# Row normalisation and rounding moved from VectorE to ScalarE in the attention units of a cross-attention and feed-forward kernel

## The reference, cut to what matters

```python
def act_quant(x):
    scale = 127.0 / jnp.clip(jnp.max(jnp.abs(x), axis=-1, keepdims=True), 1e-05)
    return jnp.clip(jnp.round(x * scale), -128, 127) / scale
...
# x: (1, 2048, 256); ctx_1024: (1, 1601, 256), masked; 4 heads of 64
x = x + xattn(ctx_1024, layernorm(x), mask, ...)   # keys and values from context and latents, softmax, W_out, bias
x = x + ffn(layernorm(x), w1, conv_w, conv_b, w2)  # bit_linear, depthwise conv of 3, silu, bit_linear
```

## Time and profile before

| | |
|---|---|
| median of 3 runs | 434.38 us (434.12 to 435.97) |
| the profiled execution | 434.61 us, of which the span from first to last instruction is 432.8 us |
| granted TensorE clock | 0.995 of full, mean over the span |
| PE busy | 404.0 us (93%) |
| DVE busy | 376.7 us (87%) |
| ACT busy | 313.9 us (73%) |
| POOL busy | 81.8 us (19%) |
| the chain that ended last | PE 49%, DVE 28%, ACT 16%, issue 3%, DMA 2% |

### The profile page before, as it was taken

How to read it: one execution, slowest core, us unless ns; L and a number is a source line. 1 busy time by engine, 2 the same in 40 slices (tenths; PEclk the granted TensorE clock), 3 DMA queues, 4 the chain that set the end, 5 groups by cost and what they waited for, 6 DMA issues and landing times.

```text
span 432.8 us, 13955 instructions
## 1 busy us (share of the span) xinstructions
PE 404.0 (93%) x5983; PEld 277.2 (64%) x5983; DVE 376.7 (87%) x604; ACT 313.9 (73%) x368; POOL 81.8 (19%) x109
## 2 busy tenths in 40 slices
PE   6999997899999999999999999999999977999894
PEld 5666674566666676676666666666676735676573
DVE  5789987977887899799799799799799899999993
ACT  2466777589979766766767767766766688999974
POOL 3287775500000020020020020020020010221200
PEclk9999999999999999999999999999999998999999
DMA  7825323711111111111111211211111000001002
GB/s 227 219 25 107 54 41 43 231 53 64 52 39 64 39 44 57 51 39 63 51 39 50 64 39 38 64 50 39 40 38 39 2 0 2 2 26 48 27 27 79
DMA packets 28688, 24.63 MB, mean 57 GB/s; under 512 B 6278, under 2 KB 28367, under 8 KB 28623
## 3 DMA queue, kind: packets, MB, share of 16 engines
q1 hardware_dynamic: 26106, 21.59, 15.6%
q0 software_dynamic: 2176, 2.10, 3.7%
q10 hardware_dynamic: 340, 0.01, 0.0%
HBM read 9.00 MB, written 2.10 MB: 26 GB/s over the span
## 4 chain that ended last, share of the span: by engine, by line
PE 49%; DVE 28%; ACT 16%; issue 3%; DMA 2%; ACTq 0%; DVEq 0%; SPq 0%
DVE arena L719 17%; PE sc L1714 10%; ACT arena L1302 5%; PE heads L1731 5%; PE heads L1732 4%; PE heads L1733 4%; PE heads L1537 4%; PE sc L1549 3%; ACT qq L1389 3%; PE sc L1814 2%; PE by L1618 2%; ACT qq L1397 2%; PE bx L1549 2%; PE by L1549 2%; ACT kk L1367 1%
## 5 line engine op out<-in xcount | busy, mean ns | idle before, releaser
L719 DVE SCALAR_TENSOR_TENSOR arena<-arena 128x1024 bf16<-128x1024 f32 x160 | 190.9, 1221 | 29.4 <-ACT arena L1302 28.2
L1302 ACT ACTIVATE arena<-sc,kb 128x1024 f32<-128x1024 f32 x160 | 169.9, 1115 | 60.9 <-PE sc L1714 60.7
L1731 PEld LDWEIGHTS heads<-v,arena 128*128 128x128 bf16 x1280 | 117.1, 97 | 41.3 <-issue 27.2
L1731 PE MATMUL heads<-v,arena 128*128 128x65 f16 x1280 | 129.8, 194 | 4.7 <-DVE arena L719 4.3
L1732 PE MATMUL heads<-v,arena 128*128 128x64 f16 x1280 | 128.9, 195 | 0.0
L1733 PE MATMUL heads<-v,arena 128*128 128x65 f16 x1280 | 128.4, 192 | 0.0
L1714 PE MATMUL sc<-qs,kst 64*128 64x512 f16 x960 | 118.0, 378 | 2.4 <-DVE kk L661 1.5
L1732 PEld LDWEIGHTS heads<-v,arena 128*128 128x128 bf16 x1280 | 118.7, 97 | 0.1
L1733 PEld LDWEIGHTS heads<-v,arena 128*128 128x128 bf16 x1280 | 118.8, 99 | 0.0
L1714 PEld LDWEIGHTS sc<-qs,kst 64*128 64x128 f16 x960 | 40.1, 94 | 47.7 <-issue 4.3
L528 POOL TENSOR_SCALAR frs<-fmv 128x2 f32<-128x2 f32 x8 | 8.0, 997 | 250.6 <-DVE fmv L793 250.6
(11 more groups left out here) (209 smaller groups left out, 582.7 us busy)
## 6 DMA issues: line engine op xcount, KB each, us to landing
kst<-kk SPq DMA_DIRECT2D x80, 128.0 KB, 2.0
xs<-in_x SPq DMA_DIRECT2D x8, 256.0 KB, 5.1
xs<-in_L_xattn_b_out POOLq DMA_DIRECT2D x8, 256.0 KB, 5.8
qs<-qq SPq DMA_DIRECT2D x16, 128.0 KB, 2.5
out<-cbuf SPq DMA_DIRECT2D x7, 256.0 KB, 2.1
xs<-in_ctx SPq DMA_DIRECT2D x6, 256.0 KB, 5.7
xs<-in_L_ffn_w SPq DMA_DIRECT2D x1, 1024.0 KB, 6.8
cbuf<-in_L_ffn_w SPq DMA_DIRECT2D x1, 1024.0 KB, 9.1
```

Of the source, the lines that this page charges most:

```text
L719: e.scalar_tensor_tensor(out=rest[:, j, :, :], in0=prob[:, j, :, :], scalar=SHRINK, in1=probh[:, j, :, :], op0=ALU.mult, op1=ALU.subtract) ...
L1302: a_.activation(prob[:, j, :, :], sc[(j + 1) % 2][:, :, :], ACT.Exp, bias=kb[:, bass.ds(i * QUAD + j, 1)]).then_inc(exp_done[j], 1)
L1731: t_.matmul(o, hi, row[:, 0:OW], start=first and sub == 0, stop=False, skip_group_check=True)
```

## The change

On DVE, `row_normed` is replaced by `row_shift`, which makes -mean x reciprocal deviation for both tiles in one small operation; the two normalising operations and the two rounding operations are issued by ACT (`row_norm`, `row_rounding`) with this bias. DVE's remaining row steps stand one or two remainders later. On ACT the normalising pair stands ahead of the exponentials of quad 3, the rounding pair between the exponentials of its tiles 2 and 3. The same is written into the branch for other numbers of quads.

```diff
-            def row_normed(b):
+            def row_shift(b):
                 dve.wait_ge(s["rstd2_ready"], b + 1)
                 settle(b)
-                for t in range(2):
-                    last = e.tensor_scalar(y[:, t, :], tile_of(b, t), fmv[:, t, 0:1], frs[:, 1, t:t + 1], ALU.subtract, ALU.mult)
-                last.then_inc(s["row_step"], 1)
+                e.scalar_tensor_tensor(out=fq[:, 3, 0:2], in0=fmv[:, 0:2, 0], scalar=-1.0, in1=frs[:, 1, 0:2], op0=ALU.mult, op1=ALU.mult).then_inc(s["row_shifted"], 1)
 
             def row_largest(b):
-                dve.wait_ge(s["row_step"], 7 * b + 1)
+                dve.wait_ge(s["row_normed"], b + 1)
+                settle(b)
                 e.tensor_reduce(fq[:, 0, 0:2], y, AX.X, ALU.max, apply_absolute_value=True).then_inc(s["row_step"], 1)
...
             def row_inverse(b):
-                dve.wait_ge(s["row_step"], 7 * b + 3)
-                e.reciprocal(fq[:, 2, 0:2], fq[:, 1, 0:2]).then_inc(s["row_step"], 1)
-
-            def row_rounded(b):
-                dve.wait_ge(s["row_step"], 7 * b + 4)
-                settle(b)
-                for t in range(2):
-                    last = e.tensor_scalar(y[:, t, :], y[:, t, :], fq[:, 2, t:t + 1], ROUND, ALU.mult, ALU.add)
-                last.then_inc(s["row_step"], 1)
+                dve.wait_ge(s["row_step"], 4 * b + 2)
+                e.reciprocal(fq[:, 2, 0:2], fq[:, 1, 0:2]).then_inc(s["row_inverted"], 1)
 
             def row_scaled_back(b):
-                dve.wait_ge(s["row_step"], 7 * b + 5)
+                dve.wait_ge(s["row_rounded"], b + 1)
...
                 remainder(first + 2, 0)
                 remainder(first + 2, 1)
+                row_shift(b)
                 remainder(first + 2, 2)
-                row_normed(b)
                 remainder(first + 2, 3)
+                remainder(first + 3, 0)
                 row_largest(b)
                 row_scale(b)
-                remainder(first + 3, 0)
+                remainder(first + 3, 1)
                 row_inverse(b)
-                remainder(first + 3, 1)
-                row_rounded(b)
                 remainder(first + 3, 2)
+                remainder(first + 3, 3)
                 row_scaled_back(b)
-                remainder(first + 3, 3)
                 row_high(b)
                 remainder(first + 4, 0)
                 row_low(b)
...
+            def row_norm(b):
+                act.wait_ge(s["row_shifted"], b + 1)
+                for t in range(2):
+                    last = a_.activation(y[:, t, :], xs[:, bass.ds(b * 2 + t, 1), :].rearrange("p a d -> p (a d)"), ACT.Identity, scale=frs[:, 1, t:t + 1], bias=fq[:, 3, t:t + 1])
+                last.then_inc(s["row_normed"], 1)
+
+            def row_rounding(b):
+                act.wait_ge(s["row_inverted"], b + 1)
+                for t in range(2):
+                    last = a_.activation(y[:, t, :], y[:, t, :], ACT.Identity, scale=fq[:, 2, t:t + 1], bias=shifts[:, 2:3])
+                last.then_inc(s["row_rounded"], 1)
+
             def unit(nq, b):
...
                 exponentials(first + 1, 1)
-                over(2, nq, lambda i: exponentials(first + i, i))
+                exponentials(first + 2, 2)
+                row_norm(b)
+                for j in range(QUAD):
+                    exponential(first + 3, 3, j)
+                    if j == 2:
+                        row_rounding(b)
+                over(4, nq, lambda i: exponentials(first + i, i))
                 rows_t(b)
```

More of the change, by code:

```diff
@@ L164, in xattn_ffn @@
         frs = sb("frs", [P, 2, 4], F32)
-        fq = sb("fq", [P, 3, 4], F32)
+        fq = sb("fq", [P, 4, 4], F32)
         fu = sb("fu", [P, 4, FT], F32)
@@ L239, in xattn_ffn @@
             rstd2_ready dq_ready xd_ps xd_ready h_ps edge_ps center_ready left_ready taps_done edge_step edge_done
-            u_ready row_step ut_ps scale_step scale_pool scale_back uscale_ready uscale_late uf_ready uqt_ps uq_ready uq_late0 uq_late1 o_ps res_ready pad_done passed""".split()
+            u_ready row_step row_shifted row_normed row_inverted row_rounded ut_ps scale_step scale_pool scale_back uscale_ready uscale_late uf_ready uqt_ps uq_ready uq_late0 uq_late1 o_ps res_ready pad_done passed""".split()
         s = {n: sem(n) for n in names}
@@ L793, in row_moments @@
                     e.bn_aggr(fmv[:, c0 + t, :], fst[:, c0 + t, :]).then_inc(s["prep_step"], 1)
-            def row_normed(b):
+            def row_shift(b):
                 dve.wait_ge(s["rstd2_ready"], b + 1)
                 settle(b)
-                for t in range(2):
-                    last = e.tensor_scalar(y[:, t, :], tile_of(b, t), fmv[:, t, 0:1], frs[:, 1, t:t + 1], ALU.subtract, ALU.mult)
-                last.then_inc(s["row_step"], 1)
+                e.scalar_tensor_tensor(out=fq[:, 3, 0:2], in0=fmv[:, 0:2, 0], scalar=-1.0, in1=frs[:, 1, 0:2], op0=ALU.mult, op1=ALU.mult).then_inc(s["row_shifted"], 1)
             def row_largest(b):
-                dve.wait_ge(s["row_step"], 7 * b + 1)
+                dve.wait_ge(s["row_normed"], b + 1)
+                settle(b)
                 e.tensor_reduce(fq[:, 0, 0:2], y, AX.X, ALU.max, apply_absolute_value=True).then_inc(s["row_step"], 1)
             def row_scale(b):
-                dve.wait_ge(s["row_step"], 7 * b + 2)
+                dve.wait_ge(s["row_step"], 4 * b + 1)
                 e.tensor_scalar(fq[:, 1, 0:2], fq[:, 0, 0:2], QUANT_EPS, 1.0 / 127.0, ALU.max, ALU.mult).then_inc(s["row_step"], 1)
             def row_inverse(b):
-                dve.wait_ge(s["row_step"], 7 * b + 3)
-                e.reciprocal(fq[:, 2, 0:2], fq[:, 1, 0:2]).then_inc(s["row_step"], 1)
-            def row_rounded(b):
-                dve.wait_ge(s["row_step"], 7 * b + 4)
-                settle(b)
-                for t in range(2):
-                    last = e.tensor_scalar(y[:, t, :], y[:, t, :], fq[:, 2, t:t + 1], ROUND, ALU.mult, ALU.add)
-                last.then_inc(s["row_step"], 1)
+                dve.wait_ge(s["row_step"], 4 * b + 2)
+                e.reciprocal(fq[:, 2, 0:2], fq[:, 1, 0:2]).then_inc(s["row_inverted"], 1)
             def row_scaled_back(b):
-                dve.wait_ge(s["row_step"], 7 * b + 5)
+                dve.wait_ge(s["row_rounded"], b + 1)
                 settle(b)
@@ L828, in row_high @@
             def row_high(b):
-                dve.wait_ge(s["row_step"], 7 * b + 6)
+                dve.wait_ge(s["row_step"], 4 * b + 3)
                 wait(dve, "xd_ps", b)
@@ L833, in row_low @@
             def row_low(b):
-                dve.wait_ge(s["row_step"], 7 * b + 7)
+                dve.wait_ge(s["row_step"], 4 * b + 4)
                 e.tensor_tensor(dq16[:, 1, :, :], y, dq16[:, 0, :, :], ALU.subtract).then_inc(s["dq_ready"], 1)
@@ L1161, in _ @@
                         remainder(first + 2, 1)
+                        row_shift(b)
                         remainder(first + 2, 2)
-                        row_normed(b)
                         remainder(first + 2, 3)
+                        remainder(first + 3, 0)
                         row_largest(b)
                         row_scale(b)
-                        remainder(first + 3, 0)
+                        remainder(first + 3, 1)
                         row_inverse(b)
-                        row_rounded(b)
-                        remainder(first + 3, 1)
+                        remainder(first + 3, 2)
+                        remainder(first + 3, 3)
                         row_scaled_back(b)
-                        remainder(first + 3, 2)
                         row_high(b)
-                        remainder(first + 3, 3)
+                        remainder(first + 4, 0)
                         row_low(b)
-                        with dve.Fori(4, nq) as i:
-                            remainders(first + i)
+                        for j in range(1, QUAD):
+                            remainder(first + 4, j)
+                        with dve.If(nq > XP // 2 + 1):
+                            with dve.Fori(5, nq) as i:
+                                remainders(first + i)
                 feed_forward()
```

## The result

The changed kernel takes 437.39 us (median; before in the same comparison 434.25), a ratio of 1.0082 with a 95% interval of 1.0063 to 1.0102: 3.6 us slower (2.7 to 4.4). The forecast was 438.5 us, slower by 4.1. The direction, the mechanism and its place came as predicted; the time lies inside the range.

A forecast was written before the change was run, and what follows sets the result against it. TensorE was taken as the bound nearly everywhere, with V4.1 setting the period; six units 0.68 us longer each gave 4.1 us, so 438.5 us, 0.95% slower, range 436.3 to 441.0 us for 8 in 10.

The forecast's parts named there:

- V4.1: TensorE's value products of quad 4, tile 1: claimed to set the unit's period and start 0.68 us later.
- The stall of 0.61 us per unit: TensorE's waits behind DVE in quads 3 and 4 before the change: 0.09 + 0.34 + 0.18 us per unit.
- The normalising pair is free: On ACT ahead of quad 3's exponentials: fits ACT's gap of 0.86 us; cost 0.03, at most 0.23.
- E3.0: ACT's exponential of quad 3, tile 0: claimed at 259.55 us, against 259.52 before.
- The shift's wait for POOL: DVE's shift in quad 2 waits for POOL's power until 257.63 us; hidden, since DVE waits until 257.68 anyway.
- The rounding pair: On ACT between quad 3's last two exponentials: idles 0.42 us for DVE's inverse, then holds ACT 1.00 us.
- E3.3: ACT's exponential of quad 3, tile 3: claimed to start at 264.93 us, 1.42 late.
- S4.1: TensorE's score products of quad 4, tile 1: claimed at 266.10 us instead of 265.41, waiting for a score bank.
- R3.3: DVE's remainder of the exponential of quad 3, tile 3: claimed at 266.07 us, after DVE idles 1.1 us.
- Faster: Rival: relieving DVE ends the stalls in quads 3 and 4, all 3.7 us comes back, 430.7 us; chance 0.09.
- No change: Rival: the two effects cancel, with quad 3's last exponential delayed near 0.75 us; 434.4 us; chance 0.06.
- Slower by more: Rival: POOL's late power delays the shift and the normalising pair too, 1.2 us per unit, 441.5 us; chance 0.05.

The follow-up runs named there:

- both eased: Changed kernel with the rounding pair behind quad 3's exponentials, and DVE's largest, reciprocal and low part each behind a later remainder; unit 32.47 us, 429.42 us, ratio 0.9910.
- DVE's order eased: Changed kernel, rounding pair left in place, DVE's high and low parts moved behind quad 4's remainders of tiles 0 and 1; unit 33.28 us, ratio 0.9982.

## Why the prediction was right

**The bound and the gate.** V4.1 set the end of the unit in both kernels, and the first five units repeat to 0.01 us (the last is 0.02 to 0.03 shorter). The stall of 0.61 us per unit that I took from the rows is borne out: the two runs without waits for remainders in quads 3 and 4 and with little or no wait at the scores are 0.59 and 0.66 shorter per unit than before.

**The normalising pair is free.** E3.0 was predicted at 259.55 on the clock of the rows before and came at 259.53 (263.32 less 3.79). The run with this half alone shows it at the end of the line: faster by 0.59 per unit.

**The shift's wait for POOL is hidden.** It stands in the waits with 0.60 us per unit, but DVE idled 0.62 in that place before, for an exponential; R2.2 comes 0.05 later (261.52 less 3.79 = 257.73). My sentence that a visible wait for POOL would show the prediction wrong was badly put: the wait is visible and harmless, because it took over an idle that was there.

**The rounding pair.** Every step of the working, on the same clock, predicted and seen: R3.0 260.68, 260.66; the inverse 263.74, 263.73; the pair 263.93, 263.92; E3.3 264.93, 264.92; S4.1 266.10, 266.07; R3.3 266.07, 266.05; scaled back 267.21, 267.19. The sign to look for was a wait of TensorE's scores of 0.7 us per unit; it reads 1.03 in the weight loads and 0.54 in the matmuls, and the scores start 0.66 late. The runs that move the pair show that this is cause and not company. One operation of the pair takes 594 ns in the units, as in the tail. The page "ScalarE: Activation LUTs" of the Trainium skill (Rules for kernel authors) gives an estimate of 0.51 us, for an operation with the bias alone as a pointer; here the scale is one as well. By the single operation its advice to keep such arithmetic on VectorE agrees with the traces, which have 594 ns on ACT and 407 ns on DVE for the normalising. For the kernel the advice is not borne out in this place: the normalising pair on ACT makes the unit 0.59 us shorter.

**The term that was mis-sized.** From the scaling back to the high part I took 0.52, as before; it is 0.64 (270.98 to 271.62). Before, a remainder stood between the two; now the second waits for the end of the first. This 0.12 is the difference between the 0.68 per unit predicted and the 0.80 measured, and it passes through every later step to V4.1, 271.19 where I had 271.08. Busy times were off as well: DVE's fell by 0.83 per unit (5 us in six, 7 forecast), and ACT's rose by 1.85 (11 us, 14 forecast), since I took the sum of durations that overlap.

**The sum.** The units alone lengthen by 6 x 0.80 = 4.8 us, more than the 4.1 forecast; the ratios say 3.6 and 2.3 us. A small part of the difference is seen at the end of the program, which the prediction took as moving as a whole. The last result on DVE, in the chain of waits before and after:

```profile
428.26 0.40 issue
428.66 0.48 DVE cbuf L957
```

```profile
433.52 0.04 issue
433.57 0.48 DVE cbuf L948
```

Between what released it and its start lie 0.40 us before, and 0.04 us in the changed kernel. This holds in both profiles of before and in all eight of kernels with a changed instruction list, whatever their speed, so about 0.4 us comes back that has nothing to do with row work: 4.8 - 0.4 = 4.4. Why the issue is quicker wasn't tried; the instruction list differs in its length on DVE and ACT, and no experiment took that apart. Reckoned so, the first ratio (3.6 us, at most 4.4) and those of the runs with either half of the change, with the rounding pair behind quad 3 and with both eased agree with their units.

Three ratios come out lower than their units say: the second one of the change (2.3 us for 4.4), the run with DVE's order eased (0.8 us faster for 0.5 slower) and the one with the pair one exponential earlier (9.1 for 11.2). All three were compared with the same 16 runs of before, which had the highest median of the three comparisons (434.73). In six of these 16 the mean granted clock was 0.985 to 0.991, and their median is 435.4; none of the 22 runs of the three kernels was below 0.994. Against the ten runs of before at 0.994 or more (median 434.16) the medians differ by 2.9, -0.2 and 9.9 us. So about 0.6 us of the lack goes with the clock, and the rest stays open.

That the time came within 1.1 us of the forecast is therefore in part luck: the units lengthened by 0.7 us more than was worked out, and the end of the program and the spread between runs took that back.

**The rivals.** "Faster" failed in the place that its deciding point named: E3.3's delay was 1.41, over 0.74; with the pair moved away from it, the gain that this rival promised is there in part (32.80), and in full with DVE's order eased too (32.47). "No change" needed a delay near 0.75 and fails by the same 1.41. "Slower by more" failed since POOL's power came in time: the shift started at 257.65 on the clock of the rows before (261.44 less 3.79). (Its sum, 434.4 + 6 x 1.2, is 441.6 and not 441.5; and "as much again" on both sides of 437.4 to 439.8 would have been wider than the 436.7 to 440.6 that I wrote. The result lies inside either.)

## What to carry to other kernels

Before moving work to an engine with idle time, look which instruction on that engine stands right behind the new one, and who waits for it. The same two operations cost nothing in a gap that the engine has in every period, and more than all that they saved when they part two instructions that feed the bound. When an operation comes with a wait on another engine, put it where that engine's result has long arrived; and on the engine that was relieved, put the operations that others wait for ahead of those that have time.

## What the runs showed that was not expected

TensorE's granted clock falls to half (1.2 GHz) for some microseconds once in the middle of the tail of every profile, and the length of the tail goes with the place. In seven of the ten profiles, among them both of the changed kernel and the second of before, it falls 13 to 15 us after the last reciprocal of the attention sums, for 3.4 us, and the last search for a largest magnitude starts 79.5 us after that reciprocal. In the first profile of before and in the run with both eased it falls at 19 us, for as long, and the same point comes at 80.4. So 0.9 us of a profile's tail goes with where the clock falls, as much as the change adds to one unit (0.80); that it is the cause wasn't tried. In the run with the normalising alone on ACT it stayed at half for about 10 us, and that tail took 92.3 us: its span (431.5) understates the gain that its ratio gives.

```profile
core 0: us, PE busy (x) PEld busy (x) DVE busy (x) ACT busy (x) POOL busy (x), PEclk, DMA share, GB/s
...
360.00:375.00 15.00, 13.59 (x116) 8.93 (x116) 14.21 (x24) 13.28 (x18) 2.88 (x9) 0.89 0.01 2
```

```profile
core 0: us, PE busy (x) PEld busy (x) DVE busy (x) ACT busy (x) POOL busy (x), PEclk, DMA share, GB/s
346.03:366.20 20.17, 16.02 (x141) 9.57 (x137) 19.03 (x48) 15.84 (x24) 1.85 (x4) 0.92 0.00 0
```

These are the stretches in the middle of the tail in which the granted clock is below 1, first of the kernel before and then of the changed one (it falls once more after TensorE's last matmul): 0.89 of 15 us and 0.92 of 20 us are each a little over 3 us at half.
